# Graph network on one core: one operand of VectorE's instructions put in PSUM in three of seven passes, and 16 instead of 14 columns picked by TensorE in one of them

## What is computed

```python
messages = x[src] * edge_probs[:, None] * weight            # layer 0
out = segment_sum(messages, dst) + x * self_loop_weight
m = einsum('ei,eio->eo', xj, W)                             # layer 1, twice: W from a small net per edge
e = leaky_relu(alpha_s[src] + alpha_d[dst], 0.2)            # layer 2, twice: 3 heads, then 1 head
m = segment_max(e, dst); p = exp(e - m[dst]); z = segment_sum(p, dst)
out = segment_sum(h[src] * (p / z[dst])[:, :, None], dst)
for r in range(8):                                          # layer 3, twice: 8 edge types
    out = out + (segment_sum(x[src] * (type == r), dst) / cnt) @ W[r]
```

## Time and profile before

| | before |
|---|---|
| median of 3 runs | 24750.14 us |
| the profiled execution | 24703.6 us |
| its span, first to last instruction | 24702.3 us |
| mean granted TensorE clock | 0.883 |
| GpSimd busy | 74% of the span, 18458 instructions |
| VectorE busy | 58% |
| TensorE (matmul) busy | 80% |

### The profile page before, as it was taken

How to read it: one execution, slowest core, us unless ns; L and a number is a source line. 1 busy time by engine, 2 the same in 40 slices (tenths; PEclk the granted TensorE clock), 3 DMA queues, 4 the chain that set the end, 5 groups by cost and what they waited for, 6 DMA issues and landing times.

```text
span 24702.3 us, 328868 instructions
## 1 busy us (share of the span) xinstructions
PE 19828.3 (80%) x124988; PEld 13345.9 (54%) x124988; DVE 14221.7 (58%) x31398; ACT 1123.5 (5%) x2172; POOL 18400.7 (74%) x18458
## 2 busy tenths in 40 slices
PE   6688778888788888766767477777689999988885
PEld 6688744444444454455555333333378887544443
DVE  6577667777667777656666534333356666333333
ACT  0000000000000000100000000000010000000000
POOL 7777777777777777777777677777757777677776
PEclk9899889999889999888888688888789999799997
DMA  5344422222122222133333222222233333222221
GB/s 155 99 131 132 118 51 54 54 54 54 41 54 54 54 54 54 37 90 99 100 102 102 59 67 72 70 71 72 63 97 112 112 113 106 53 58 59 59 58 42
DMA packets 1190681, 1902.10 MB, mean 77 GB/s; under 512 B 398267, under 2 KB 766709, under 8 KB 1180669
## 3 DMA queue, kind: packets, MB, share of 16 engines
q1 hardware_dynamic: 596752, 1670.28, 20.0%
q0 software_dynamic: 590528, 209.38, 8.6%
q10 hardware_dynamic: 1837, 1.39, 0.0%
HBM read 1258.97 MB, written 620.63 MB: 76 GB/s over the span
## 4 chain that ended last, share of the span: by engine, by line
POOL 72%; issue 22%; PE 3%; DVE 1%; DMA 0%; SPq 0%; ACT 0%; DVEq 0%; ACTq 0%; POOLq 0%
POOL gb L516 70%; PE psB L811 1%; POOL ext L531 1%; POOL ext L506 1%; PE psA L800 1%; SPq L338 0%; PE psB L829 0%; PE psB L834 0%; DVE Sb L1104 0%; PE psB L687 0%; DVE prod L1139 0%; PE psA L823 0%; DVE prod L1429 0%; DVE prod L1424 0%; ACT prod L584 0%
## 5 line engine op out<-in xcount | busy, mean ns | idle before, releaser
L687 PE MATMUL psB<-xp,arena 128*128 128x224 bf16 x58170 | 6007.3, 264 | 688.1 <-DVE arena L1007 620.0
L687 PEld LDWEIGHTS psB<-xp,arena 128*128 128x128 bf16 x58170 | 5701.0, 100 | 1443.3 <-issue 820.6
L687 PE MATMUL psB<-ext,arena 128*128 128x280 bf16 (+1 forms) x20874 | 3376.7, 325 | 1238.0 <-DMA arena<-oh_d 1223.6
L749 PE MATMUL psB<-w2as,hid 128*128 128x512 f32 x6448 | 3298.3, 643 | 845.3 <-DVE prod L1139 845.3
L687 PEld LDWEIGHTS psB<-ext,arena 128*128 128x128 bf16 x20874 | 2092.5, 101 | 2488.1 <-DMA arena<-oh_d 1253.6
L516 POOL DMA_INDIRECT gb<-tab2b,srci x2604 | 2720.4, 1045 | 793.6 <-issue 793.6
L516 POOL DMA_INDIRECT gb<-tab1b,srci x2728 | 2636.2, 966 | 848.8 <-issue 831.1
L516 POOL DMA_INDIRECT gb<-tab1a,srci x2728 | 2633.7, 965 | 842.8 <-issue 831.1
L516 POOL DMA_INDIRECT gb<-tab3b,typi x2604 | 2492.8, 957 | 913.7 <-issue 793.3
L516 POOL DMA_INDIRECT gb<-tab2a,srci x2356 | 2610.3, 1108 | 718.2 <-issue 718.2
L1139 DVE TENSOR_TENSOR prod<-psB,gb 128x1024 f32<-128x1024 f32 x1612 | 1974.1, 1225 | 1829.0 <-PE psB L749 953.1
(11 more groups left out here) (315 smaller groups left out, 15979.8 us busy)
## 6 DMA issues: line engine op xcount, KB each, us to landing
arena<-oh_d SPq DMA_DIRECT2D x1324, 448.0 KB
oh_d<-arena SPq DMA_DIRECT2D x558, 448.0 KB
hid<-oh_d SPq DMA_DIRECT2D x515, 448.0 KB
ext<-oh_d SPq DMA_DIRECT2D x207, 448.0 KB
S2a<-Sb SPq DMA_DIRECT2D x62, 1404.0 KB
S2b<-Sb SPq DMA_DIRECT2D x62, 884.0 KB
S3a<-Sb SPq DMA_DIRECT2D x62, 832.0 KB
gb<-tab1a,srci POOLq DMA_INDIRECT x2728
```

Source lines behind the costliest of these rows:

```text
L687: m = pe.matmul(psB[b][:, u * 512:u * 512 + W], pk.onehot(n)[:, g, u * P:(u + 1) * P], pk.part(g, i), start=g == 0 and i == 0, stop=g == N ...
L749: m = pe.matmul(psB[g % 2][:, i * 512:(i + 1) * 512], hid[:, o:o + P], w2as[:, :], start=True, stop=True)
```

## The change

Three things. (1) In passes 0, 3 and 4, small rows that VectorE's two-input instructions read are held in `psA` and no longer in SBUF: the column's slice of `same` (`pssame`), the edge weights (`psew`), the lists 0 to 7 and 0 to 13 (`psio8`, `psio14`), the logits `raw`, the decay `d0`, and ScalarE's exponentials, which it now writes to `psA[1]`. Copies of 52 elements (or of the lists, once for each pass) are added for that. (2) `edge_weight` writes its comparison to PSUM. (3) `OFF[3]` goes from 14 to 16: over `tab2a` 36 positions of a column are gathered and 16 picked, so 8 pairs and not 7.

```diff
-OFF = (18, 8, 8, 14, 10, 16, 10)
+OFF = (18, 8, 8, 16, 10, 16, 10)
...
+        pssame, psew, psio8, psio14 = (psA[0][:, o:o + n] for o, n in ((0, TC), (TC, TC), (2 * TC, 8), (2 * TC + 8, JB)))
+        PZ, PD = 128, 288
...
-                    a.activation(da, da, ACT.Exp).then_inc(a_exp, 1)
+                    a.activation(psA[1][:, 0:2 * TC * H], da, ACT.Exp).then_inc(a_exp, 1)
...
+                spots = psio14 if pk.k in (0, 3, 4) else io14
                 v.tensor_tensor(v3(hm[:, 0:pk.off * JB], JB), bc(hlk[:, (c + 1) * KM - pk.off:(c + 1) * KM], 2, JB),
-                                bc(io14, 1, pk.off), ALU.is_equal)
+                                bc(spots, 1, pk.off), ALU.is_equal)
...
+            def lists_to_psum():
+                v.tensor_copy(psio8, io8)
+                v.tensor_copy(psio14, io14)
...
             def weighted_pass():
+                lists_to_psum()
...
+                    v.tensor_copy(psew, ewc[:, s * TC:(s + 1) * TC])
+                    v.tensor_copy(pssame, same[:, span(c)])
                     arrived(0, c)
                     v.drain()
...
-                    v.tensor_tensor(pr[:, :, 0:16], got(c, 16), bc(ewc[:, s * TC:(s + 1) * TC], 2, 16), ALU.mult).then_inc(d_gbfree, 1)
-                    done = sums(0, c, 16, done, range(24), lambda q: pr[:, :, q], lambda q: same[:, span(c)])
+                    v.tensor_tensor(pr[:, :, 16:24], bc(typi[:, span(c)], 2, 8), bc(psio8, 1, TC), ALU.is_equal)
+                    v.tensor_tensor(pr[:, :, 0:16], got(c, 16), bc(psew, 2, 16), ALU.mult).then_inc(d_gbfree, 1)
+                    done = sums(0, c, 16, done, range(24), lambda q: pr[:, :, q], lambda q: pssame)
...
+                raw, d0 = psA[0][:, PZ:PZ + TC * H], psA[0][:, PD:PD + TC * H]
+                decay3, weight3 = (v3(psA[1][:, i * TC * H:(i + 1) * TC * H], H) for i in range(2))
...
+                    v.tensor_copy(pssame, same[:, span(c)])
                     v.drain()
                     for i in used:
-                        m = v.tensor_tensor_scan(xs[:, :, i], same[:, span(c)], xe[:, :, i],
+                        m = v.tensor_tensor_scan(xs[:, :, i], pssame, xe[:, :, i],
...
-                    v.scalar_tensor_tensor(e, zz, 0.2, zz, ALU.mult, ALU.max)
+                    v.scalar_tensor_tensor(raw, zz, 0.2, zz, ALU.mult, ALU.max)
...
-                    v.tensor_tensor(v3(d0, H), e3, bc(same[:, span(c)], 2, H), ALU.mult)
+                    v.tensor_tensor(d3, decay3, bc(same[:, span(c)], 2, H), ALU.mult)
                     for h in range(H):
-                        v.tensor_copy(pr[:, :, h * w], p3[:, :, h])
-                        m = v.tensor_tensor(pr[:, :, h * w + 1:(h + 1) * w], gv[:, :, 0:D], bc(p3[:, :, h], 2, D), ALU.mult)
+                        v.tensor_copy(pr[:, :, h * w], weight3[:, :, h])
+                        m = v.tensor_tensor(pr[:, :, h * w + 1:(h + 1) * w], gv[:, :, 0:D], bc(weight3[:, :, h], 2, D), ALU.mult)
...
-                    done = sums(k, c, width, done, range(H, f), lambda q: pr[:, :, q - H], lambda q: v3(d0, H)[:, :, (q - H) // w])
+                    done = sums(k, c, width, done, range(H, f), lambda q: pr[:, :, q - H], lambda q: d3[:, :, (q - H) // w])
```

More of the change, by code:

```diff
@@ L1151, in softmax_pass @@
                 pk = PICK[k]
-                zz, d0, nb = sub[:, 0:TC * H], sub[:, TC * H:2 * TC * H], sub[:, 2 * TC * H:2 * TC * H + TC]
+                zz, nb = sub[:, 0:TC * H], sub[:, 2 * TC * H:2 * TC * H + TC]
+                raw, d0 = psA[0][:, PZ:PZ + TC * H], psA[0][:, PD:PD + TC * H]
+                decay3, weight3 = (v3(psA[1][:, i * TC * H:(i + 1) * TC * H], H) for i in range(2))
+                r3, d3 = v3(raw, H), v3(d0, H)
                 da = sub[:, TC * 7:TC * (7 + 2 * H)]
                 e, p = da[:, 0:TC * H], da[:, TC * H:2 * TC * H]
-                z3, e3, p3 = v3(zz, H), v3(e, H), v3(p, H)
+                z3, p3 = v3(zz, H), v3(p, H)
                 xes = [v3(arena[:, i * TC * 12:i * TC * 12 + TC * ef], ef) for i in range(2)]
@@ L1179, in softmax_pass @@
                     v.drain()
-                    v.scalar_tensor_tensor(e, zz, 0.2, zz, ALU.mult, ALU.max)
+                    v.scalar_tensor_tensor(raw, zz, 0.2, zz, ALU.mult, ALU.max)
                     v.drain()
                     for h in range(H):
-                        v.tensor_tensor_scan(now[:, :, h], nb, e3[:, :, h], old[:, TC - 1, h:h + 1] if c else -BIG, ALU.add, ALU.max)
+                        v.tensor_tensor_scan(now[:, :, h], nb, r3[:, :, h], old[:, TC - 1, h:h + 1] if c else -BIG, ALU.add, ALU.max)
                     done = picks(k, done, pk.until(c, 0.3), width)
@@ L1190, in softmax_pass @@
                         v.memset(z3[:, 0, :], 0.0)
-                    v.tensor_tensor(p3, e3, now[:, :, 0:H], ALU.subtract)
+                    v.tensor_tensor(p3, r3, now[:, :, 0:H], ALU.subtract)
                     v.drain()
@@ L1195, in softmax_pass @@
                     v.wait_ge(a_exp, NCH * (k - 3) + c + 1)
-                    v.tensor_tensor(v3(d0, H), e3, bc(same[:, span(c)], 2, H), ALU.mult)
+                    v.tensor_tensor(d3, decay3, bc(same[:, span(c)], 2, H), ALU.mult)
                     for h in range(H):
-                        v.tensor_copy(pr[:, :, h * w], p3[:, :, h])
-                        m = v.tensor_tensor(pr[:, :, h * w + 1:(h + 1) * w], gv[:, :, 0:D], bc(p3[:, :, h], 2, D), ALU.mult)
+                        v.tensor_copy(pr[:, :, h * w], weight3[:, :, h])
+                        m = v.tensor_tensor(pr[:, :, h * w + 1:(h + 1) * w], gv[:, :, 0:D], bc(weight3[:, :, h], 2, D), ALU.mult)
                     m.then_inc(d_gbfree, 1)
-                    done = sums(k, c, width, done, range(H, f), lambda q: pr[:, :, q - H], lambda q: v3(d0, H)[:, :, (q - H) // w])
+                    done = sums(k, c, width, done, range(H, f), lambda q: pr[:, :, q - H], lambda q: d3[:, :, (q - H) // w])
                     done = picks(k, done, pk.until(c, 1), width)
             def edge_weight(c, xs):
-                oh = v3(prod[:, 0:TC * 8], 8)
+                of_type, oh = v3(psA[1][:, 0:TC * 8], 8), v3(prod[:, 0:TC * 8], 8)
                 tc = typi[:, span(c)]
-                v.tensor_tensor(oh, bc(tc, 2, 8), bc(io8, 1, TC), ALU.is_equal)
+                v.tensor_tensor(of_type, bc(tc, 2, 8), bc(psio8, 1, TC), ALU.is_equal)
                 v.drain()
-                v.tensor_tensor(oh, oh, xs[:, :, 4:12], ALU.mult)
+                v.tensor_tensor(oh, of_type, xs[:, :, 4:12], ALU.mult)
                 v.scalar_tensor_tensor(tc, srci[:, span(c)], 8.0, tc, ALU.mult, ALU.add)
```

1 line of the change is left out of this document (removed).

## The result

The changed kernel takes 23891.35 us, the median of 4 runs (23888.78 to 23892.41), against 24751.27 us, the median of 4 runs of the kernel before (24705.97 to 24761.54). The ratio is 0.9656, with a 95% interval of 0.9639 to 0.9673: 860 us less by the medians, 811 us by the two profiled executions (24703.6 and 23892.41).

The account below looks back on a forecast made before the run. It took GpSimd's gathers, at 1.249 us each, as the bound; 155 + 371 + 254 + 38 - 3 = 815 us off gave 23889 profiled, 23935 median. Forecast 23910, range 23820 to 24220.

Parts of the forecast that it names:

- 124 gathers, at 1.249: Over tab2a, 124 fewer gathers on POOL at a pace of 1.249 us each: 155 us off.
- excess over tab2a: Gather busy time over tab2a above 0.944 us each, 386 us; 371 forecast to go with operands in PSUM.
- excess over tab2b: Gather busy time over tab2b above 0.944 us each, 262 us; 254 forecast to go.
- excess over in_x: Gather busy time over in_x above 0.944 us each, 76 us; half, 38, forecast to go.
- last column, lists: VectorE's extra work showing at tab2a's last column, and copying the lists three times: 3 us added.
- the four short instructions with two inputs in SBUF: L1180, L1186, L1188, L1210, left unchanged: 1.2 us a column over tab2a, 0 to 48 us of excess staying.
- The one gather of the earlier trace, at 0.94: Gather of 0.94 us beside seven TENSOR_SCALARs with a pointer scalar in SBUF, taken to show that pointers hold nothing.
- the pointer of a scan: Rival: scans still hold gathers because their start value points into SBUF; 390 us off, 24340; chance 0.08.
- the copies: Rival: short copies in a two-port mode hold gathers, not two inputs; 285 us off at most, 24450 to 24600; chance 0.04.
- PSUM's price: Extra VectorE time for an operand in PSUM, taken as 0 from a 224-element product at 392 ns either way.
- VectorE's cover over `tab2a`: VectorE's slack in a tab2a column: 38.6 us of work under POOL's pace of 45.2, 6.6 us.
- the rival of TensorE's pace: Rival: TensorE's matmul pairs, with an eighth added, pace tab2a; 24000 to 24300 us; chance 0.10.

Follow-up runs that it names:

- run 23892: The profiled execution of the changed kernel itself, with nothing further changed; 23892.41 us, against 24703.6 for the profiled execution of the kernel before.
- The run with drains: Kernel before, all inputs in SBUF, plus a VectorE drain after each segment-sum scan over tab2a and tab2b; 24337.42 us, ratio 0.9809.
- r4_rest_psum: Changed kernel with 14 picked columns over tab2a and the segment sums' decay back in SBUF; 24557.18 us, ratio 0.9914 against the kernel before.

## Why the prediction was right

**The bound.** GpSimd's gathers set the time, and what a gather costs was the question. This is shown: the stages' differences add up to 810 of 811 us, and the idle time within a pass is still only "issue".

**The sum.** Against the profiled execution the sum gave 23889 and the run 23892. Part of that closeness is luck, since errors of 5 to 21 us in single terms partly cancel:

| term | forecast, us | measured, us |
|---|---|---|
| 124 gathers, at 1.249 | 155 | 155 |
| excess over tab2a | 371 | 386 |
| excess over tab2b | 254 | 262 |
| excess over in_x | 38 | 30 |
| last column, lists | -3 | about 0 |
| tab1a, tab1b | 0 | -21 |
| tab3a, tab3b | 0 | -5 |

What I kept back for the four short instructions with two inputs in SBUF (15 and 8 us) was not lost at all: the longest gather over `tab2a` is 1018 ns. The run with drains fits this: there the segment sums, one scan at a time, delay a gather by 0.11 us at most. Over `tab1a` and `tab1b`, whose code is the same, gathers were 14 and 7 us longer than before. In the kernel with drains, whose code for them is the same as before, it is 16 and 6 (2650.0 and 2642.1 against 2633.7 and 2636.2), so it takes no operand in PSUM to bring it about. Nearly all of it lies at scans, which read two tensors from SBUF in these passes (72 us over `tab1a`, 57 before). What moved it was not tested.

Over `in_x` the forecast took half of the excess by choice, and 46 us stayed, for a reason that it did not have. Some 12 us lie at seven gathers beside a two-input instruction at the start of the pass (L917). Another 25 us lie at gathers beside the runs of TENSOR_SCALAR (L1009), which read one tensor and a pointer scalar: 346 gathers that have nothing else of VectorE beside them are 15 us longer in all, by up to 0.12 us each. The one gather of the earlier trace rows, at 0.94, was not typical of them.

**The median.** I took the middle between 23889 (profiled) and 23935 (moved by the 46.5 us that lay between the profiled execution and the median). The offset was not carried over: the changed kernel's four runs lie within 3.6 us. That is the 19 us by which the forecast was too high. The kernel with drains still shows the offset (24273 profiled, the others 24333 to 24344), the four kernels with freed products don't. These few runs show it and do not explain it.

**The cause.** The conclusion "an instruction that reads two tensors from SBUF holds up a gather; one that reads a tensor from PSUM does not, nor does a pointer" held for the scans and products of this change, and its rivals fell: the pointer of a scan (the scans keep it, and gathers among them take 0.94), and the copies (they read PSUM with the scans' decay back in SBUF, and 291 us stay). As a rule it is wrong at both ends. With both inputs in SBUF and a drain between scans nearly all of the delay at the scans is gone too; what holds a gather for long is an unbroken stretch of such work, a run of scans or one product of 1 to 2 us. And one tensor with a pointer is not free everywhere: the runs of TENSOR_SCALAR over `in_x` cost up to 0.12 us a gather. The Trainium skill's remark that a `tensor_tensor` did not stall DMA issue in its probe ("SBUF — State Buffer", section "Who interferes with whom") doesn't agree with these rows: beside a product of 1.89 us, with no copy near, a gather took 2.39 us. The remark may hold for short ones; it was not tried.

**PSUM's price.** I took 0 by one row. A scan with its decay in PSUM takes 313 ns, and in `r4_rest_psum`, where the same scans read it from SBUF, 313 as well (5124 scans, 1205.9 us); the product of 832 elements takes 1009 ns, and 1.02 us with both inputs in SBUF. Only the copy of 52 elements became dearer, 249 ns for 218, 8 us in all and hidden. VectorE's cover over `tab2a` was forecast as 6.6 us a column and is 7.3, over `tab2b` 24 and 23.8.

**TensorE.** The margin was forecast as 2.3 us a column (42.9 of 45.2); the row shows 2.88 us of idle time, before a load of one-hots, and the stage's busy time gives 2588.93 / 62 = 41.8 us of a column of 44.95. The eighth pair fitted, as the rival of TensorE's pace said it might not. One more would not fit by these numbers: a pair takes 5.1 us and a column would shrink to 34 x 1.249 = 42.5 us. That is an estimate, and was not tried on an ordinary chip.

## What to carry to other kernels

When gathers pace a kernel, compare the mean with the median of the same gather over different stages: the difference, times the count, is what another engine costs it, and the timeline at the longest ones shows what ran beside them. Here it went by giving long or unbroken VectorE work one operand in an idle PSUM bank, at no price in VectorE's time. Before a resource is freed, ask what keeps up with it only because it was held: on two of the four chips the same freed gathers cost 4 to 5%.

## What was not expected of the hardware

- A drain between two-input scans restores the gathers among them (excess over `tab2a` from 386 to 112 us, time down by 475 us), though it makes 22 scans 8.79 us long instead of 5.17.
- Two of the chips ran the kernel before in 38233 and 37884 us, against 24769 and 24813 on the others. Gathers took the same time, 943 ns at best; TensorE fell from 235 to 17 matmuls in 28 us where gathers came at full pace, with a granted clock of 1.00 (the level of 2.4 GHz) in the first stretch and 0.57, near the level of 1.2 GHz, in the second. The clock is not what is missing: TensorE is busy for 5.71 us of the second stretch and idle for 22, with single matmuls 1.4 and then 2.8 us apart.
